# Four layers of cross-attention and feed-forward on one core: quantised mixtures in pairs, layer 2 with three score banks and a ring of five

## Time and profile before

| | us |
|---|---|
| median of 3 runs | 2365.03 (2362.05 to 2366.44) |
| profiled execution | 2363.66 |
| its span | 2361.9 |
| PE busy | 2141.9 (91%) |
| DVE busy | 1444.6 (61%) |
| ACT busy | 1210.7 (51%) |
| POOL busy | 608.3 (26%) |
| stages, starts in the span | L0a 4.8, L0f 436.0, L1a 501.9, L1f 807.1, L2a 928.8, L2f 1809.9, L3a 1885.5, L3f 2310.3 |

### The profile page before, as it was taken

One profiled execution on the slowest core, in us unless ns is written; L12 is line 12 of the kernel. 1 busy time (PEld: TensorE's weight loads), 2 busy tenths in 40 slices (PEclk: granted clock), 3 DMA queues, 4 the chain that ended last, 5 costly groups with the idle time before them and its releaser, 6 DMA issues. The chain is left out here.

```text
span 2361.9 us, 48903 instructions
## 1 busy us (share of the span) xinstructions
PE 2141.9 (91%) x19446; PEld 1587.3 (67%) x19446; DVE 1444.6 (61%) x3160; ACT 1210.7 (51%) x2347; POOL 608.3 (26%) x233
## 2 busy tenths in 40 slices
PE   6999999448999697899999999999996889999995
PEld 3777777336888553577777777777773447777773
DVE  5777777568888344555544554455533667777775
ACT  5777787204666231244444444444430367777761
POOL 6656553015656100600000000000000054353400
PEclk8999999658999798799999999999997979999996
DMA  6554453022432012100000000000000154444420
GB/s 168 141 148 136 140 151 87 14 79 78 128 114 72 19 36 62 42 17 18 29 22 17 17 24 27 17 18 17 1 1 10 44 154 141 133 145 124 126 63 17
DMA packets 87073, 165.20 MB, mean 70 GB/s; under 512 B 40384, under 2 KB 48624, under 8 KB 86592
## 3 DMA queue, kind: packets, MB, share of 16 engines
q1 hardware_dynamic: 86848, 162.08, 23.7%
HBM read 81.75 MB, written 0.46 MB: 35 GB/s over the span
## 5 line engine op out<-in xcount | busy, mean ns | idle before, releaser
L1540 PEld LDWEIGHTS L2ps<-L2values,L2probsT 125*128 125x128 f32 (+1 forms) x2688 | 317.5, 192 | 50.6 <-issue 49.6
L1521 PE MATMUL L2ps<-L2keys,L2qz 128*128 128x501 f32 x672 | 340.0, 589 | 0.9 <-DVE L2out_bias L1784 0.9
L1540 PE MATMUL L2ps<-L2values,L2probsT 125*128 125x128 f32 (+1 forms) x2688 | 318.4, 275 | 0.0
L1737 DVE CUSTOM_DVE_ANT_0 L2work<-L2ps,L2maskadd,L2big 128x1503 f32<-128x1503 f32 x112 | 199.7, 1783 | 163.2 <-PE L2ps L1521 163.2
L122 POOL TENSOR_TENSOR rstd<-mv,half_neg 112x8 f32<-112x8 f32 x9 | 16.8, 1866 | 972.1 <-DVE mv L138 972.1
L1535 PEld LDWEIGHTS L2ps<-const,L2work 128*126 128x126 f32 x1344 | 163.8, 140 | 116.5 <-issue 64.9
L647 ACT ACTIVATE L3probsT<-L3ps 128x448 f32<-128x448 f32 x384 | 196.0, 547 | 70.8 <-PE L3ps L504 66.0
L647 ACT ACTIVATE L0probsT<-L0ps 128x448 f32<-128x448 f32 x384 | 198.1, 551 | 48.0 <-PE L0ps L504 46.8
L1535 PE MATMUL L2ps<-const,L2work 128*126 128x128 f32 x1344 | 202.2, 273 | 1.8 <-ACT L2work L1661 1.0
L1652 ACT ACTIVATE L2z<-L2ps,L2rinv 128x128 f32<-128x128 f32 x112 | 41.1, 367 | 304.8 <-PE L2ps L1540 304.8
L791 DVE TENSOR_REDUCE L3partmax<-L3ps 112x1 f32<-112x1000 f32 x128 | 153.4, 1198 | 58.3 <-PE L3ps L477 56.3
(11 more groups left out here) (463 smaller groups left out, 4194.3 us busy)
## 6 DMA issues: line engine op xcount, KB each, us to landing
L0key_stack<-L0key_parts SPq DMA_DIRECT2D x192, 187.5 KB
L3key_stack<-L3key_parts SPq DMA_DIRECT2D x192, 187.5 KB
L0ctxT<-in_ctxT SPq DMA_DIRECT2D x16, 750.0 KB, 4.2
L1raw<-in_ctx SPq DMA_DIRECT2D x16, 750.0 KB
L1rawT<-in_ctxT SPq DMA_DIRECT2D x16, 750.0 KB, 5.7
L2raw<-in_ctx SPq DMA_DIRECT2D x16, 750.0 KB
L3ctxT<-in_ctxT SPq DMA_DIRECT2D x16, 750.0 KB, 4.5
L1fw<-in_L_w SPq DMA_DIRECT2D x16, 256.0 KB, 2.8
```

What stands on the lines that cost most here:

```text
L1521: last = nc.tensor.matmul(PS[:, 3 * (m % 2) + c, 0:NPR], tile_rows(m), KT[:, m // RT % 2, 500 * c:500 * c + NPR], start=True, stop=True)
L1540: last = nc.tensor.matmul(PS[:, bank, 0:P], PT[0:keys_in(c), i % 2, c, :], V[0:keys_in(c), i // RT % 2, c, :], start=c == 0, stop=c == NCH ...
L1737: nc.vector.tensor_tensor_reduce(SM[:, m % 2, :].rearrange("p (c n) -> p c n", c=3), PS[:, 3 * (m % 2):3 * (m % 2) + 3, 0:NPR], MA[:, m // ...
```

## The change

- The norm goes in two halves of four tiles through all its steps, with one power per half. Twice normed x is normed once, with both epsilons folded into the variance.
- Loads ahead: L0f's and L3f's weights are loaded at the end of the attention before them, L1a's weights, first two contexts and masks in L0f, L2a's weights in L1f.
- L0f: ACT takes the weight sums and one scaling of them, and the rounding of gelu's output; DVE makes the factors of two tiles at once; rings of four; PE's order is written for pairs. L3f: sums and scaling on ACT, half of the copies on ACT, the first down product between the turns of the second half.
- L1a: the latents' products come first, all keys and values of batch 0 behind them, batch 1's after the first scores; copies and squares go partly to ACT.
- L1f: POOL scales and centres L2a's weights in slices of four heads (24 operations) and makes the 16 powers for the context; DVE makes two sums.
- L2a: the scores of one tile in three banks and a ring of five for the units; on PE whole runs: three chunks, then T, T, T, O. The inverse sum scales the probabilities (DVE, 1503 columns) and no longer the output. O has its operands swapped, so that the output comes feature-major and no Z is left. The keys of batches 1 to 15 are no turned values: they are loaded feature-major, together with the context's means and scales spread over the partitions (through a DRAM scratch), and POOL subtracts and multiplies.

```diff
 def ln_dve(dve, k, s, ps, link, eps, scale=None, bias=None, feature_major=True, meanwhile=None):
...
+    for h in range(2):
+        tiles = range(4 * h, 4 * h + 4)
+        dve.wait_ge(s.ln_tok, h + 1)
...
+        if len(eps) == 1:
+            last = nc.vector.tensor_scalar(var, var, eps[0], None, ALU.add)
+        else:
+            last = nc.vector.tensor_scalar(var, var, 1.0 + eps[1], eps[0] * eps[1], ALU.mult, ALU.add)
+        last.then_inc(s.ln_var, 1)
+    if meanwhile:
+        meanwhile(0)
+    for h in range(2):
+        dve.wait_ge(s.ln_rstd, h + 1)
...
 def latent_attention(nc, k, src, ahead):
...
             last.then_inc(s.lat_v, 1)
-            for what, j in (("K", 0), ("V", 0), ("K", 1), ("V", 1)):
-                unit(what, 1, j)
...
             scores(0, range(4))
+            for j in range(3):
+                unit("K", 1, j)
+                unit("V", 1, j)
...
             key_norm(0)
+            deviations(1)
             deviations(2)
             key_norm(1)
...
+class WideAhead:
...
+        for n in (1, 2):
+            for g in range(4):
...
+                nc.gpsimd.tensor_tensor(self.products[:, n - 1, heads], w, row(1), ALU.mult).then_inc(s.products, 1)
+                pool.wait_ge(s.products, 4 * n + g - 3)
+                nc.gpsimd.tensor_tensor(w, w, row(0), ALU.mult).then_inc(s.scaled, 1)
+                pool.wait_ge(s.scaled, 4 * n + g - 3)
+                nc.gpsimd.tensor_tensor(w[:, :, 0:P - 1], w[:, :, 0:P - 1], w[:, :, P - 1:P].to_broadcast([64, 4, P - 1]),
+                                        ALU.subtract).then_inc(s.centred, 1)
+        pool.wait_ge(s.ve_ready, 1)
+        for b in range(B):
+            nc.gpsimd.tensor_tensor(self.rs[:, b, :], self.rs[:, b, :], self.k.half_neg[0:CH, 0:NCH], ALU.pow).then_inc(s.spread, 1)
...
 class WideHeadUnits:
...
-        return 6 + self.place[what] % 2
+        return 3 + self.place[what] % 5
...
 def attention_16_wide_heads(nc, k, src, ahead):
...
+                for rows in (slice(0, TT), slice(TT, P - 1)):
+                    sp.dma_start(KT[rows, b % 2, 0:S2], src["ctxT"][b][rows]).then_inc(s.key_parts, 16)
+                for x, to in enumerate((MEAN[:], SCALE_OF)):
+                    sp.dma_start(to, scratch[x, b].rearrange("c n -> (c n)").partition_broadcast(P)).then_inc(s.key_parts, 16)
...
-                    for c in range(NCH):
-                        last = nc.tensor.matmul(PS[:, bank, 0:P], PT[0:keys_in(c), i % 2, c, :], V[0:keys_in(c), i // RT % 2, c, :],
+                        last = nc.tensor.matmul(PS[:, bank, 0:P], V[0:keys_in(c), i // RT % 2, c, :], PT[0:keys_in(c), i % 2, c, :],
...
             for n in range(plan.last_step + 1):
+                if n + 1 < RT * B:
+                    for c in range(3):
+                        scores(n + 1, c)
+                for u in (plan.first(n), plan.second(n), plan.third(n), plan.output(n)):
+                    if u:
+                        unit(*u)
...
+            for b in range(1, B):
+                pool.wait_ge(s.key_parts, 64 * b)
+                nc.gpsimd.tensor_tensor(KT[0:P - 1, b % 2, 0:S2], KT[0:P - 1, b % 2, 0:S2], MEAN[0:P - 1], ALU.subtract
+                                        ).then_inc(s.keys_moved, 1)
+                pool.wait_ge(s.keys_moved, b)
+                nc.gpsimd.tensor_tensor(KT[0:P - 1, b % 2, 0:S2], KT[0:P - 1, b % 2, 0:S2], SCALE_OF[0:P - 1], ALU.mult
+                                        ).then_inc(s.keys_scaled, 1)
...
+            def scale(m):
+
+                dve.wait_ge(s.exp_done, m + 1)
+                nc.vector.reciprocal(rinv[:, m % 4:m % 4 + 1], ssum[:, m % 4:m % 4 + 1]).then_inc(s.rinv_ready, 1)
+                dve.wait_ge(s.rinv_ready, m + 1)
+                nc.vector.tensor_scalar(PR[:, m % 2, :], PR[:, m % 2, :], rinv[:, m % 4:m % 4 + 1], None, ALU.mult
+                                        ).then_inc(s.scaled, 1)
...
             for n in range(plan.last_step + 1):
                 b, t = divmod(n, RT)
+                if n + 1 < RT * B:
+                    maximum(n + 1)
                 if plan.first(n):
                     empty(*plan.first(n))
...
+                if n + 1 < RT * B:
+                    scale(n + 1)
...
 def bitlinear_ffn(nc, k, src, weights, ahead=None):
...
+            for t in range(6):
+                up(t)
+            turn(0)
+            turn(1)
+            up(6)
+            up(7)
+            for p in range(1, 4):
+                down(2 * p - 2)
+                turn(2 * p)
+                down(2 * p - 1)
+                turn(2 * p + 1)
...
+            def quantise(p):
+                act.wait_ge(s.factor_ready, p + 1)
+                for t in (2 * p, 2 * p + 1):
...
+                    nc.scalar.activation(Gr[:, t % 4, :], Gl[:, t % 4, :], ACT.Identity, bias=magic[0:TT], scale=rxs[:, 1, t:t + 1]
+                                         ).then_inc(s.gq_ready, 1)
...
+            for p in range(4):
+                if p < 3:
+                    pre(2 * p + 2)
+                    pre(2 * p + 3)
+                factors(p)
+                if p:
+                    keep(2 * p - 2)
+                    keep(2 * p - 1)
```

More of the change, by code:

```diff
@@ L1333, in _ @@
             last.then_inc(s.lat_done, 1)
-            empty("K", 1, 2)
             empty("T2", 0, 1)
+            maximum(0)
+            for j in range(3):
+                empty("K", 1, j)
             stats(2)
@@ L1374, in __init__ @@
         for n in range(self.last_step + 1):
-            self.units += [u for u in (self.first(n), self.second(n), self.extra(n), self.third(n), self.output(n)) if u]
+            self.units += [u for u in (self.first(n), self.second(n), self.third(n), self.output(n)) if u]
         self.place = {u[:3]: i for i, u in enumerate(self.units)}
@@ L1510, in _ @@
                 load_mask(b)
+                load_keys(b)
         @block.tensor
@@ L1908, in _, with gelu @@
+            pe.wait_ge(s.wq_ready, 1)
+            for t in range(6):
[9 more added lines that the diff above has]
+                turn(2 * p + 1)
+            turn_back(0)
+            down(6)
+            down(7)
+            turn_back(1)
         @block.scalar
         def _(act):
-            for t in range(NTT):
+            def gelu(t):
@@ L1916, in _ @@
+            weights.wait(act)
+            weight_sums(nc, s, H, wsum, W)
+            act.wait_ge(s.scales_ready, 2)
+            for n in range(2):
+                nc.scalar.activation(W[:, n, :], W[:, n, :], ACT.Identity, scale=rws[:, n:n + 1]).then_inc(s.w_scaled, 1)
+            for p in range(4):
+                gelu(2 * p)
+                gelu(2 * p + 1)
+                if p:
+                    quantise(p - 1)
+            quantise(3)
         @block.vector
@@ L2248, in _, with ternary_ffn @@
                 up(e)
+                if ahead and e == 2:
+                    ahead.variances()
+                if ahead and e in (5, 6):
+                    ahead.vector(dve, link, e - 4)
                 gated(e)
-def ternary_ffn(nc, k, src):
+def ternary_ffn(nc, k, src, weights):
     F, NF = 512, 4
@@ L2284, in _, with up @@
         def _(pe):
-            ln_pe(pe, k, s, ps)
-            pe.wait_ge(s.sums_ready, 1)
-            nc.tensor.matmul(ps[:, 7, 0:2], k.ones[:], wsum[:], start=True, stop=True).then_inc(s.sums_total, 1)
-            pe.wait_ge(s.ln_done, 2)
-            pe.wait_ge(s.wq_ready, 1)
-            for t in range(NTT):
+            def up(t):
                 if t >= 4:
@@ L2310, in _ @@
                 last.then_inc(s.y_ready, 1)
+            ln_pe(pe, k, s, ps, feature_major=False)
+            pe.wait_ge(s.sums_ready, 2)
+            nc.tensor.matmul(ps[:, 7, 0:2], k.ones[:], wsum[:], start=True, stop=True).then_inc(s.sums_total, 1)
+            ln_turn(pe, k, s, ps)
+            pe.wait_ge(s.wq_ready, 1)
+            for h in range(2):
+                pe.wait_ge(s.ln_done, h + 1)
+                for t in range(4 * h, 4 * h + 4):
+                    up(t)
+            pe.wait_ge(s.wq_ready, 2)
+            for h in range(2):
+                pe.wait_ge(s.norm_ready, h + 1)
+                for c in range(NF):
+                    turn(h, c)
+                    if h and c == 1:
+                        down(0)
+            down(1)
         @block.scalar
         def _(act):
+            weights.wait(act)
+            weight_sums(nc, s, hT, wsum, W)
+            act.wait_ge(s.scales_ready, 1)
+            for n in range(2):
+                nc.scalar.activation(W[:, n, :], W[:, n, :], ACT.Identity, scale=rws[:, n:n + 1]).then_inc(s.w_scaled, 1)
             for t in range(NTT):
@@ L2316, in _ @@
                 nc.scalar.activation(G[:, t, :], ps[0:TT, 4 + t % 4, :], ACT.Gelu).then_inc(s.gelu_done, 1)
+            for n in range(0, 2 * NF, 2):
+                h, c = divmod(n, NF)
+                act.wait_ge(s.turned, n + 1)
```

(2 more changed lines are left out.)

753 lines of the change are left out of this document (380 added, 373 removed).

## The result

The changed kernel took 2254.8 us (median of 4 runs, 2252.9 to 2259.4) where the kernel before took 2363.7: a ratio of 0.954, with an interval of 0.952 to 0.956. 2263 had been predicted, with 2240 to 2292 as range. The profiled execution took 2252.9 us, its span is 2250.8; the span before was 2361.9.

The account below looks back on a forecast made before the run. TensorE was taken to bound layer 2's tile loop, chains through several engines the other changed stretches. Terms of -25, -8, -1.3, -11, -20.5, +2, -31, -1, +4, -11 and +1 gave -102: 2263 us from 2365.03, range 2240 to 2292.

Parts of the forecast that it names:

- L0f: Quantised mixture: tiles in pairs, rounding off VectorE, earlier start; 65.9 us becomes about 40.5, -25 (bounds -28 and -20).
- L1a: Start of layer 1's attention: early loads, single norm pass, later batch 1 work; -11 us (-16 to -4).
- the likeliest case: Whole kernel: the forecast itself, 2263 us, own range 2248 to 2280; chance 0.70.
- Norms: Layer norms in halves: 2.8 off 11.2 us each, three on the path, -8 in all.
- The give-back: Layer 1's attention: half the earlier first scores' gain is lost, since batch 1's key norm now follows them.
- Preparation of layer 2: Before layer 2's first scores: weights ready at the barrier, norm one pass; 51.6 for 72.1 us, -20.5 (-24 to -16).
- The loop: Layer 2's tile loop: key turns and Z's turns back gone, -31 us; with +2, -1 and +4, -26.
- The sign of 728 to 735 us: Layer 2's loop: the length that would show the forecast right; above 750 us would show it wrong.
- (b): Layer 2's loop: POOL and VectorE collide in each of 15 batches, or keys come late; 20 us more, 2284; chance 0.12.
- (c): Starts of L0f and layer 1's attention give less: half of 36 us lost, 2281; chance 0.10.
- (d): TensorE in the loop: runs save changes between kinds, 0.15 us a tile; 17 more, 2246; chance 0.05.
- (e): Layer 2's loop: TensorE waits for the scaled probabilities in every tile; slower, say 2400 us; chance 0.03.

Follow-up runs that it names:

- the broken runs: Against the changed kernel, a tile's three score products issued inside another tile's output product instead of as one run behind it; 2257.2 us.

## Why the prediction was right, and where its terms were off

The sign and the likeliest case held, and each large term came with its sign: 102 us were summed, 108.8 came between the medians and 111 between the two traces. That the sum is closer than its terms is partly luck: L0f and layer 2's preparation gave 11.5 us more than said, and the loop, L1a and L3a 8.0 less. The order of the terms did not hold: the loop was to give most, and it came third, behind L0f and the preparation.

- **L0f** gained 29.2 for 25. The first product is 12.8 us in (13.5 predicted), and from there to the end it is 23.9 (26.3). VectorE's part of a pair is 1.49 + 1.21 + 1.24 + 0.72, so 4.7 for the 4.8 of the sum, with the absmax of two tiles a little under two single ones. The rest was the allowance for waits: VectorE waits 0.9 us for the turns where it waited 8.8. That VectorE sets this stage is shown by the rounding put back. (13.5 and 26.3 make 39.8, not the 40.5 that the prediction went on with.) Its groups, as in the earlier trace rows:

```profile
L2053 DVE TENSOR_REDUCE L0fxs<-L0fgelu 112x2 f32<-112x1024 f32 x4 | 4.8, 1209 | 0.0
L2063 DVE TENSOR_SCALAR L0fgqT<-L0fps 128x448 bf16<-128x448 f32 x8 | 4.7, 618 | 0.9 <-PE L0fps L1938 0.9
```

- **Norms**: 3.5, 3.0 and 3.6 for 2.8 each. The run with one power shows 1.9 to 2.5 us of it as the split power's. What the turns back and copies gave was not taken apart.
- **L1a**: -9.2 for -11; the traces that leave this stage alone lie between -9.2 and -12.5. The first scores came 2.1 us later than laid out. GpSimd's roots were ready at 500.5, but VectorE was in batch 1's statistics until 503.0, which stand ahead of the multiplication in its queue; the step overlooked that. The give-back came as described: 18.2 gained at the first scores, 9 left at the turned keys of batch 1.
- **L1f**: nothing for GpSimd's work, as said. Its 16 powers ended at 854.7 (2.26 us each, 2.3 predicted), 28 us before the last product:

```profile
L1434 POOL TENSOR_TENSOR L2rs<-L2rs,half_neg x16: 2257/2260/2316, 818.9 to 852.5; 125x12 f32<-125x12 f32 x16
```

- **Preparation of layer 2**: the step that was furthest off, 7.3 us. "First fold near 3, its end near 10 (7.19 us as before)": it began 1.4 in, ended 5.2 in, and the query product came 7.6 in, not 13. The 7.19 was a duration at half clock, taken over into a kernel where TensorE no longer idles 19.6 us before it. Of the 7.4 us (44.2 for 51.6) the fold's own length is 3.4, its earlier start 1.6, the turns and copies 0.4, and 2.0 lie behind the query product's start. The kernel with one power, which did begin at half clock, has its fold from 2.7 to 9.9 in and its query product at 12.4, and took 50.6 where 51.6 was predicted. The Trainium skill ("TensorE: Matmul & The Clock Gate", What's actually happening) has it that a TensorE without work falls to 1.2 GHz and work releases it. The delayed fold agrees, and so does 0.71 becoming 0.95; which of two starts behind the same 2.95 us comes out full, no run here tells.
- **The loop**: -23.3 for -26. 6.52 us a tile, the reordering worth nothing and 1.5 us to spare all stood. The collision was put at 4 and cost 7.4 in this trace, 7 to 14 in others; without it (739.35) the loop gives 30.7, and the other terms say 30. The scaling took 1.00 for 0.93. The sign of 728 to 735 us was set for a stretch of 759 us before; for the 770.0 of this cut it means 739 to 746, and 750 becomes 761.
- **L3a**: -1.3 was predicted, and +2.2 came. The traces of the changed code scatter by 3.4 us around the 424.8 of before (424.0 to 427.4), so neither is shown. **L3f**: -12.1 for -11, its first product 8.0 us in for 8.6; the traces that leave it alone say -9.6 to -12.1. The +1 for more semaphore groups is not seen: TensorE's waits at the seven barriers are 17.0 us before and 16.6 after.
- **The ends**: the bounds of the prediction add up to 2314 and 2247, not to its 2308 and 2238. The forecast does not rest on them.

Of the rivals, (b) had the mechanism in full, where the forecast had it at +4: in 14 of 15 batches the scaling stood for GpSimd's product. But only meetings that last longer than the 1.5 us reach TensorE, so the price was 7 to 14 and not 20. The Trainium skill ("SBUF — State Buffer", Who interferes with whom) says that the waiting engine is blocked for the whole instruction of the other; the 4.07, 4.20 and 3.96 us agree. (c) fell with its two terms, L0f and L1a, at 38.4 us for 36, (d) with the broken runs, (e) with 0.34 us of wait after two added passes.

## What to carry to other kernels

Take a duration from the trace together with the granted clock at which it ran: if the change removes the idle time ahead of it, its length changes too. Where GpSimd works beside a chain of VectorE's that has some time to spare, cut GpSimd's instructions until one is shorter than that time; here three pieces (1.24 us each, with 1.5 to spare) cost TensorE nothing. And measure a small edit by its stage, since whole times move by several us with where the collisions fall.
